# Experts' down product as a stacked one-pass product, with the split of its weights, the rank products and the masks rearranged

## What is computed

```python
xn = layernorm(x)
logits = xn @ router_w
scores = softmax(logits)
topk_idx = top_k(logits + router_bias, 4)          # 4 experts a token
comb = topk_scores / topk_scores.sum()             # their weights
g = silu(einsum('nd,edf->nef', xn, wg))
u = einsum('nd,edf->nef', xn, wu)
routed = einsum('ne,nef,efd->nd', comb, g * u, wd) # wd is the down product
shared = (silu(xn @ swg) * (xn @ swu)) @ swd
out = x + attention(xn) + routed + shared
```

## Time and profile before

| | us |
|---|---|
| median of 3 runs (1752.04 to 1755.01) | 1753.86 |
| the profiled execution, its own time | 1752.27 |
| its span, first to last instruction | 1750.5 |
| PE busy | 1709.8 (98%) |
| DVE busy | 1308.6 (75%) |
| ACT busy | 720.2 (41%) |
| POOL busy | 607.3 (35%) |
| DMA moved | 316.02 MB, mean 181 GB/s |

### The profile page before, as it was taken

The page is one execution under the profiler, slowest core; times in us unless marked ns, Lnnn a source line. Parts: engine busy times, 40 slices in busy tenths (PEclk is TensorE's granted clock), DMA queues, the critical chain, the costliest instruction groups (busy, mean ns, idle before and its releaser), DMA issues.

```text
span 1750.5 us, 34484 instructions
## 1 busy us (share of the span) xinstructions
PE 1709.8 (98%) x11705; PEld 1513.5 (86%) x11705; DVE 1308.6 (75%) x2590; ACT 720.2 (41%) x1331; POOL 607.3 (35%) x826
## 2 busy tenths in 40 slices
PE   6999999999999999999999999999999999999997
PEld 5888899899988888888888888889999999999996
DVE  7888788888776676666667667668888888876666
ACT  4333443434344444444444444443434343434331
POOL 2333155555343333433333343333333323210011
PEclk9999999999999999999999999999999999999998
DMA  6666444344478888878888787854444444331234
GB/s 219 217 218 232 139 137 150 129 147 134 151 235 255 243 247 251 247 243 245 251 249 249 244 256 238 256 170 134 124 125 125 129 117 139 103 113 51 78 99 133
DMA packets 283501, 316.02 MB, mean 181 GB/s; under 512 B 37696, under 2 KB 233280, under 8 KB 283328
## 3 DMA queue, kind: packets, MB, share of 16 engines
q1 hardware_dynamic: 211008, 175.34, 32.7%
q0 software_dynamic: 33792, 88.13, 16.7%
q10 hardware_dynamic: 38528, 50.34, 8.1%
HBM read 169.21 MB, written 144.46 MB: 179 GB/s over the span
## 4 chain that ended last, share of the span: by engine, by line
PE 73%; DMA 12%; DVE 5%; POOL 4%; issue 4%; ACT 1%; SPq 0%; DVEq 0%; ACTq 0%; POOLq 0%
DMA rows_turned<-xz 12%; PE bank L1251 6%; PE bank L1293 6%; PE bank L1252 6%; PE bank L1253 6%; PE bank L1276 5%; PE bank L1231 5%; PE bank L1233 5%; PE bank L1232 5%; PE bank L1296 5%; PE bank L1284 5%; POOL xsT L582 4%; PE bank L1307 3%; PE bank L1305 3%; PE bank L1306 3%
## 5 line engine op out<-in xcount | busy, mean ns | idle before, releaser
L582 POOL DMA_DIRECT2D xsT<-rows_turned x384 | 210.3, 554 | 388.4 <-DMA rows_turned<-xz 378.3
L1251 PE MATMUL bank<-wh,xh 128*128 128x256 f32 x1024 | 293.9, 287 | 0.0
L1253 PE MATMUL bank<-wh,xl 128*128 128x256 f32 x1024 | 289.1, 282 | 0.0
L1252 PE MATMUL bank<-wl,xh 128*128 128x256 f32 x1024 | 288.9, 282 | 0.0
L680 ACT ACTIVATE kv<-bank 128x512 f32<-128x512 f32 x256 | 153.1, 598 | 224.4 <-PE bank L1253 224.4
L593 POOL DMA_INDIRECT yk<-slot_y,pos x128 | 131.7, 1029 | 260.5 <-DVE xr L1005 171.2
L1039 DVE STREAM_TRANSPOSE kz<-kv 128x512 f32<-128x512 f32 x127 | 90.2, 710 | 166.0 <-issue 149.0
L1251 PEld LDWEIGHTS bank<-wh,xh 128*128 128x128 f32 x1024 | 193.3, 189 | 19.2 <-issue 15.9
L1231 PE MATMUL bank<-xh,wh 128*128 128x512 f32 x512 | 208.9, 408 | 0.0
L1055 DVE SCALAR_TENSOR_TENSOR og<-tg,bank 128x512 f32<-128x512 f32 x128 | 88.0, 687 | 155.0 <-ACT o L706 155.0
L1293 PE MATMUL bank<-sm,kv 128*128 128x128 f32 x1024 | 197.9, 280 | 4.7 <-DVE sm L1019 4.4
(11 more groups left out here) (165 smaller groups left out, 3692.2 us busy)
## 6 DMA issues: line engine op xcount, KB each, us to landing
keys_turned<-kz SPq DMA_DIRECT2D x127, 256.0 KB, 2.9
kT_by_group<-keys_turned SPq DMA_DIRECT2D x508, 64.0 KB
slot_x<-zeros ACTq DMA_DIRECT2D x8, 3072.0 KB, 10.2
xs<-slot_x SPq DMA_DIRECT2D x96, 256.0 KB, 3.8
we<-wexp_in SPq DMA_DIRECT2D x192, 128.0 KB, 3.0
rows_turned<-xz POOLq DMA_DIRECT2D x96, 256.0 KB, 4.1
xsT<-rows_turned POOLq DMA_DIRECT2D x384, 64.0 KB, 3.0
slot_y<-ys ACTq DMA_DIRECT2D x96, 256.0 KB, 3.9
```

Of the source, the lines that this page charges most:

```text
L582: pool.dma_start(xsT[q % 2][b * TB:(b + 1) * TB, :, :, :].rearrange("p a k j -> p a (k j)"), xz_back[q % 2, b]).then_inc(xsT_loaded[q % 2] ...
L1251: pe.matmul(dst, lh, rh, start=(k == 0), stop=False)
L1252: pe.matmul(dst, lh, rl, start=False, stop=False)
L1253: mm = pe.matmul(dst, ll, rh, start=False, stop=(k == KD - 1))
```

## The change

It has four parts.

1. **Experts' down product.** In the first phase the down weights of all 64 experts are split into a high part (ScalarE, `high_down`) and a rest (VectorE, `low_down`), 16 pieces of four experts in groups 1 to 6, and stored in DRAM stacked, 64 rows of high part above 64 rows of rest (`wd_split`). `wd` of an expert is then 128 x 256, twice the bytes. The product `h` of gate and up is made for both experts of a pair by one instruction; ScalarE copies its high part `hh` twice, above and below; VectorE makes the rest `hl` above, and zeros stand below. A down product is two one-pass products on the whole array, `hh` and `hl` against the stacked weights, for each expert; both experts' results go into bank 6, and one copy takes them out. TensorE's order becomes ... queries, scores, `down(q0)`, `gate_up(q0 + 1)` ....
2. **Queues.** SP's `load_experts` becomes `load_up` (waits for `gate_up` two pairs earlier) and `load_down` (waits for `down` two pairs earlier); the loads of `xs` go to GpSimd's queue; `xz` is doubled, its DRAM copy has four places, and GpSimd stores two pairs before it loads two. VectorE's two `turn_rows` stand together at the start of a slot.
3. **Routing.** Masks of all blocks are kept; they and the counts are made by additions of bf16 data in place of reductions. The rank products move from the first phase to slots 1, 4, ... 22 (`slot_numbers`) and add the expert's first tile (`base_bf`); `upper` carries this number to slot numbers directly, so that picking and summing happens once. `lc` is made on ScalarE (`below_top`) and its exponential moves to slot 2.
4. **Residual.** `res4` is a ScalarE copy of the down product; the residual rows are loaded again as `xx` in the combining slots and added there on VectorE (`add_rows`).

The diff, cut to its core:

```diff
-    xz_dram = nc.dram_tensor("rows_turned", [2, P, BLK, 4 * TB], F32, kind="Internal").ap()
+    xz_dram = nc.dram_tensor("rows_turned", [4, P, BLK, 4 * TB], F32, kind="Internal").ap()
+    wd_split = nc.dram_tensor("expert_down_split", [E, P, D], F32, kind="Internal").ap()
-        wd = [keep(f"wd{i}", [P, D]) for i in range(2)]
-        hT = keep("hT", [P, P])
+        wd = [keep(f"wd{i}", [P, 2, D]) for i in range(2)]
+        hh = keep("hh", [P, 2 * P], F32R)
+        hl = keep("hl", [P, 2 * P], F32R)
...
+        def pieces(g):
+            return range(min(3 * (g - 1), PIECES), min(3 * g, PIECES)) if g >= 1 else range(0)
...
# SyncE
+            def load_piece(t):
+                sp.wait_ge(swl_ready, 2)
+                if t >= 3:
+                    sp.wait_ge(wds_stored[t % 3], 64 * (t // 3))
+                sp.dma_start(whl[t % 3][:, 1], wd_piece[t]).then_inc(wdraw_loaded[t % 3], 16)
+            def store_piece(t):
+                sp.wait_ge(wdl_ready, t + 1)
+                for m in range(2):
+                    for c in range(2):
+                        sp.dma_start(wd_parts[t, m, c], whl[t % 3][c * F:(c + 1) * F, :, m, :]).then_inc(wds_stored[t % 3], 16)
             def group(g):
+                if g < NSB - RING:
+                    sp.wait_ge(xn_ready, CH * (g + 1))
+                    sp.dma_start(xin[g % RING][:], x_grp[g + RING]).then_inc(x_loaded[g % RING], 16)
                 if g < NSB - 1:
                     store_rows(g + 1)
-                sp.wait_ge(part_ready, CH * (g + 1))
-                if g < NSB - RING:
-                    sp.dma_start(xin[g % RING][:], x_grp[g + RING]).then_inc(x_loaded[g % RING], 16)
+                for t in pieces(g):
+                    store_piece(t)
+                for t in pieces(g + 1):
+                    load_piece(t)
+                sp.wait_ge(part_ready, 2 * (g + 1))
...
+            def load_up(q):
...
+                    sp.wait_ge(gu_mm, q - 1)
+            def load_down(q):
...
+                    sp.wait_ge(y_mm, q - 1)
+                for j in range(2):
+                    sp.dma_start(wd[q % 2][:, j, :], at(wd_split, expert_of[q % 2, j])).then_inc(pair_loaded[q % 2], 16)
...
                 if EXPERT0 < s <= EXPERT1:
-                    pair_done(q0 - 1)
+                    load_down(q0 + 1)
+                if experts:
+                    load_up(q0 + 2)
                 if 1 <= s < NSTEP:
                     store_keys(s)
-                if EXPERT0 - 1 <= s < EXPERT1:
-                    load_rows(q0 + 4)
                 if experts:
-                    pair_done(q0)
+                    load_down(q0 + 2)
+                    load_up(q0 + 3)
                 if 1 <= s < NSTEP:
                     load_keys(s)
...
# GpSimd
+            for a in range(0, NPAIR, 2):
+                for q in (a, a + 1):
+                    store_turned(q)
+                    load_pair_rows(q + 2)
+                for q in (a, a + 1):
+                    load_turned(q)
...
# ScalarE, first phase
                 gate(0)
                 high(0)
+                high_down(0)
                 gate(1)
+                below_top(g)
                 high(1)
+                high_down(1)
...
+                for h in range(2):
+                    act.wait_ge(down_mm, 2 * g + h + 1)
+                    act.copy(res4[:, 2 * h:2 * h + 2, :].rearrange("p c d -> p (c d)"), bank[6 + h][:]).then_inc(part_ready, 1)
...
# ScalarE, slots
+            def high_h(q):
+                act.wait_ge(h_ready, q + 1)
+                act.wait_ge(y_mm, q)
+                for j in range(2):
+                    act.copy(hh[j * F:(j + 1) * F, :], sg[0:F, :]).then_inc(hh_ready, 1)
...
                 if experts:
                     copy_kT(s - 1)
-                    result(q0)
+                    high_h(q0)
                 if projects:
                     silu_q(s)
                 if experts:
+                    result(q0)
+                    silu_pair(q0 + 1)
                     store_result(q0)
-                    silu_pair(q0 + 1)
+                    high_h(q0 + 1)
...
# VectorE, first phase
                 shared_low(0)
                 shared_low(1)
+                low_down(0)
                 shared(2)
-                    dve.tensor_reduce(mask[:], oh[:].rearrange("p (c k) e -> p c e k", k=TOPK), AX.X, ALU.add).then_inc(mask_ready, 1)
+                link(dve.tensor_tensor(oh2[:], oh4[:, :, 0:2, :], oh4[:, :, 2:4, :], ALU.add))
                 shared_low(2)
+                dve.tensor_tensor(masks(g), oh2[:, :, 0, :], oh2[:, :, 1, :], ALU.add).then_inc(mask_ready, 1)
+                low_down(1)
                 shared(3)
                 shared_low(3)
-                dve.wait_ge(rank_mm, g + 1)
...
+                low_down(2)
...
# VectorE, slots
             def gated(q):
-                for j in range(2):
-                    dve.tensor_tensor(hT[j * F:(j + 1) * F, :], sg[F:2 * F, j * P:(j + 1) * P],
-                                      bank[7][F:2 * F, j * P:(j + 1) * P], ALU.mult).then_inc(hT_ready, 1)
+                dve.tensor_tensor(sg[0:F, :], sg[F:2 * F, :], bank[7][F:2 * F, 0:2 * P], ALU.mult).then_inc(h_ready, 1)
+            def low_h(q):
+                dve.wait_ge(hh_ready, 2 * q + 1)
+                dve.tensor_tensor(hl[0:F, :], sg[0:F, :], hh[0:F, :].bitcast(F32), ALU.subtract).then_inc(hl_ready, 1)
...
                 if projects:
                     decay_keys(s)
-                if EXPERT0 <= s + 1 < EXPERT1:
-                    turn_rows(q0 + 3)
+                if experts:
+                    low_h(q0)
+                if experts:
+                    decay_scores(s - 1)
                 if delivers:
                     add_out(s - 2, 0)
...
# TensorE
             def gate_up(q):
-                pe.wait_ge(ys_ready, q)
+                pe.wait_ge(h_ready, q)
             def down(q):
-                pe.wait_ge(hT_ready, 2 * (q + 1))
+                pe.wait_ge(hh_ready, 2 * (q + 1))
+                pe.wait_ge(hl_ready, q + 1)
+                pe.wait_ge(ys_ready, q)
                 for j in range(2):
-                    ps = slice(j * F, (j + 1) * F)
-                    mm = pe.matmul(bank[6 + j][:, 0:D], hT[ps, :], wd[q % 2][ps, :], start=True, stop=True)
+                    dst, w = bank[6][:, j * D:(j + 1) * D], wd[q % 2][:, j, :].bitcast(F32R)
+                    pe.matmul(dst, hh[:, j * P:(j + 1) * P], w, start=True, stop=False)
+                    mm = pe.matmul(dst, hl[:, j * P:(j + 1) * P], w, start=False, stop=True)
+            def slot_numbers(q):
+                pe.wait_ge(base_ready, 1)
+                pe.wait_ge(pos_ready, q)
+                for c in range(CH):
+                    o = bank[7][:, c * E:(c + 1) * E]
+                    pe.matmul(o, upper[:], mask(q * CH + c), start=True, stop=False)
+                    for j in range(c):
+                        pe.matmul(o, ones_bf[:], mask(q * CH + j), start=False, stop=False)
+                    if q > 0:
+                        pe.matmul(o, ones_bf[:], counts[:, q - 1, :], start=False, stop=False)
+                    mm = pe.matmul(o, ones_bf[:], base_bf[:], start=False, stop=True)
...
+                if ROUTE0 <= s < ROUTE0 + 3 * NSB and (s - ROUTE0) % 3 == 0:
+                    slot_numbers((s - ROUTE0) // 3)
...
                 if experts:
+                    scores(s - 1)
                     down(q0)
-                    scores(s - 1)
                     gate_up(q0 + 1)
```

## The result

The changed kernel takes 1727.62 us (median of 4 runs, 1724.67 to 1728.48) against 1753.9 before: a ratio of 0.985, 95% interval [0.984, 0.987], 26.3 us less. The forecast was 1720, 33.5 less by its sum, the range 1708 to 1744. The profiled execution took 1726.95 with a span of 1725.2; the span fell by 25.3.

The account below looks back on a forecast made before the run. TensorE was taken to bound the kernel from 196 us on. Expert slots -35, routing +6 and -0.5, first phase -4 sum to -33.5 us, from 1753.9 to 1720; range 1708 to 1744.

Parts of the forecast that it names:

- Expert slots, TensorE: Expert slots: one-pass full-array down products and shorter steps around them save 0.73 us a slot, 35 us over 48 slots.
- surroundings stay: Expert slots: steps around the new products stay long, 0.30 us a slot remains, 1741 us; chance 0.16 shared with late arrivals.
- f32 price: Expert slots: new down products still cost as much as f32 ones, about 1842 us; chance 0.01.
- the Trainium skill's rule in the prediction: Expert down products: two 64-row tiles give up to twice the throughput, a gain the new form would lose.
- Expert slots, cover of the h chain: First pair of each expert slot: hl ends near +3.5 us, down group due at +3.9, so 0.4 us spare.
- Queues: Expert slots: loads behind SP's new waits delay the keys about 1 us; unpriced, counted with the late h chain.
- DMA bound: Expert slots: doubled down weights make DMA the limit, decisive at share 0.87 (about 1757 us), 1806 at 0.81; chance 0.07.
- Routing slots: Eight routing slots: 18 rank products a block add 0.75 us each, +6 us, ends 4 and 9; VectorE gives -0.5.
- First phase: Before slot 0: shorter TensorE waits ahead of the down products, partly given back to pieces, -4 us, ends -9 and +5.
- The part without pieces: First phase: groups with no piece of down weights to split gain 1.2 us each, in about 2.7 groups.
- The fourth rival: First phase: late pieces hold ScalarE, 5 groups x 3 us = 15, 1735 us; chance 0.16 shared with other cases.
- Combining slots: Combining slots: one 128x256 VectorE addition a slot costs nothing, at most +3 us.

## Why the prediction was right, point by point

The time came in its range, and by the mechanism that was to carry it, the expert slots on TensorE. That it came so near owes something to luck: two terms were missed, and one unforeseen gain hid one of them.

- **Expert slots, TensorE: right, the gain a little too small.** 0.87 a slot against 0.73 taken, 0.79 at the most; the 0.08 above is the scores, which take 0.81 where I took 0.89; the down products run at 0.12 as forecast, and the steps around them are as short as where no 64-row product stands. The runs with half the products show that this form, not the f32 price, lengthened them. The rivals "surroundings stay" and "f32 price" fall. The halves did work side by side: in the kernel before, the instructions of the two experts start in pairs 6 to 7 ns apart in all 96 groups (906.512 and 906.518, then 906.832 and 906.838), 0.31 us for a pair. That agrees in kind with the Trainium skill's rule in the prediction (TensorEngine Tiling (Array Packing), section Overview); twice the throughput is not shown. So the new form did give that up, and won by fewer passes and by its neighbours. Whether 64-row one-pass products on opposite halves would have done better, no run here shows.
- **Expert slots, cover of the h chain: right, but thinner than it looks.** `hl` ends 0.37 us (median of 48, 0.10 at the least) before its down group; 0.4 was forecast. The view of waits has none on `hl` or `hh`. But the run with the longer chain shows that 0.10 of it is the hand-over, and that six slots have nothing left, about 1 us in all.
- **Queues: the step that failed in this stage.** I asked who stands behind SP's new waits and named the keys. The other answer was one line away: the loads that were moved behind the down group still count into the semaphore on which `gate_up` waits. And the view behind the earlier trace rows had the sign of it in its second line, four such waits of 1.8 us together, where the prediction says that TensorE hardly waited for a landing. It cost 12.6 us, almost hidden in the sum: with the semaphore of its own the stretch is 45.1 us shorter than before, 10 more than I took, 5 of them by the medians of the slots and a part because the waits of the kernel before went as well.
- **DMA bound: the rival falls.** 0.87 was to decide; the run with the semaphore of its own held 0.96 and 284 GB/s over 635 us, where the earlier trace rows had 0.93 over 7, without a single wait of TensorE.
- **Routing slots: right sign, half the size.** The 18 rank products take 0.54 us in place of 0.75: in one block they start at 270.86, and the next step at 271.40. They follow each other at 0.03. Seven blocks at 0.53 and the first, with 14 products, at 0.42 make 4.1; the stage grew by 3.2, and the 0.9 between is not traced to a step.

```profile
270.86 0.20 PE L1445 MATMUL bank<-mask_a,upper 128*128 128x64 bf16 x1
270.90 0.19 PE L1449 MATMUL bank<-counts,ones_bf 128*128 128x64 bf16 x1
...
271.40 0.47 PE L1389 MATMUL bank<-kv,kp 128*128 128x128 f32 x2
```

- **First phase: wrong sign.** The part without pieces was right: -10.1 us in the run with one piece, and 1.2 in each of eight blocks is -9.6. The pieces' instructions were priced at 5.1 and cost 3.0. The term that was mis-sized is the transfers, which I had at nothing in the sum and only as an end of the range: 11.5 us, of which up to 5.1 are the clock at 0.50 in three stretches (an estimate, half of 3 x 3.4). The fourth rival, late pieces at 3 us in five blocks, had the mechanism and, at 15 us, something near the size; its mark, ScalarE's waits on the pieces, is in the trace with 5.9 us, and I gave it too small a share of the sum. No row of before showed that round trip; the row of after is SP's, whose issue of a group's 12 stores takes 9.6 to 12.4 us of some 22 (11.7 in group 2), with the next loads queued behind. The clock was nowhere in the prediction.
- **Combining slots: right**, +0.8.

## What to carry to other kernels

A load that is moved must have its semaphore moved with it: look at every wait that counts it, not only at the one that needs it. A short wait in a view is a sign of what will grow: read the view to its last line. Work that depends on a transfer belongs behind the critical chain in each engine's order, even where the engine is idle most of the time, since its wait stops all that stands after it. And a product that leaves part of the array unused is to be priced with its neighbours: what it costs shows in the steps before and after it.

## What the runs showed of the hardware

- Two 64-row one-pass products of 256 columns in the same half of the array took 0.43 us where two of 128 rows took 0.32 and 0.24, and the neighbouring 128-row steps were 0.10 to 0.17 longer. Two f32 products in opposite halves started 6 to 7 ns apart, 0.31 us for each pair of instructions.
- TensorE's granted clock fell to 0.50 (1.2 GHz) for 3.4 us at waits of 1.9, 2.4, 2.4 and 2.6 us, and did not after another of 2.4 (at 168.80 in the first phase), nor after one of 1.85 in the kernel before. With most of each wait filled it stayed at 1.00.
- SP needed 11.73 us to issue twelve stores of 64 partitions, 0.98 each, while the DMA engines' share was 1.00 (78.6 to 90.4); a pair of loads of `wd` took 0.88 (median) in the expert slots, 0.44 each, though some pairs took two to three times that.
- Additions of bf16 masks on VectorE took 0.41 us (128x512) and 0.28 (128x256), those of f32 and fp32r pieces of 128x512 0.68.
- A share of 0.96 of the DMA engines was sustained for 635 us.
- The four loads of a pair count into one semaphore in both kernels. The Trainium skill, DMA: Bandwidth & Descriptors, section Why a DMA increments its semaphore by 16 and not by 1, asks for one semaphore for each buffer in flight, for the sake of correct data, which no run here touches. What the runs show is that giving `wd` its own is worth 12.6 us of the expert slots in one execution each, and some 11 us of the whole by the ratios (0.985 and 0.979).
